# Twelve key-tile steps of row maxima ahead instead of sixteen, in a four-layer graph network on one core

## The reference, cut to what matters

```python
# L2 (adj is 0 or 1 here)
logits = jnp.einsum('bhqd,bhkd->bhqk', q, k) / np.sqrt(DK)
logits = logits + jnp.log(jnp.clip(adj, ADJ_MIN, None))[:, None, :, :]
attn = jax.nn.softmax(logits, axis=-1)
out = jnp.einsum('bhqk,bhkd->bhqd', attn, v)
# L3
logits = jnp.einsum('bhnd,bhmd->bhnm', q, k) / math.sqrt(Hd)
logits = logits + (2.0 * adj - 1.0)
weights = jax.nn.softmax(logits, axis=-1)
weights = weights * (0.25 + 0.75 * adj)
weights = weights / jnp.maximum(weights.sum(axis=-1, keepdims=True), 1e-06)
attended = jnp.einsum('bhnm,bhmd->bhnd', weights, v)
```

## Time and profile before

| | |
|---|---|
| median of 3 runs | 4452.08 us (4448.81 to 4457.96) |
| profiled execution | 4446.08 us, its span 4444.3 us |
| TensorE busy | 4062.8 us, 91% of the span |
| VectorE busy | 3042.6 us, 68% |
| ScalarE, GpSimd busy | 2204.3 us (50%), 1917.8 us (43%) |
| TensorE's granted clock, mean | 0.957 of full speed |

### The profile page before, as it was taken

The page is one execution under the profiler, slowest core; times in us unless marked ns, Lnnn a source line. Parts: engine busy times, 40 slices in busy tenths (PEclk is TensorE's granted clock), DMA queues, the critical chain, the costliest instruction groups (busy, mean ns, idle before and its releaser), DMA issues.

```text
span 4444.3 us, 69344 instructions
## 1 busy us (share of the span) xinstructions
PE 4062.8 (91%) x21040; PEld 2185.1 (49%) x21040; DVE 3042.6 (68%) x5152; ACT 2204.3 (50%) x3894; POOL 1917.8 (43%) x1064
## 2 busy tenths in 40 slices
PE   7998999989999899998999989998999989999898
PEld 6534465344753447543474434744347443574335
DVE  3797746877478764787647876478755787557874
ACT  3365533655336553365534655246543465435663
POOL 1174602746027560265503655036540465404562
PEclk9998999999999999999999999999999999999999
DMA  3201102011020110201112011120111101111010
GB/s 107 77 18 34 51 21 67 18 34 51 25 63 18 34 51 30 60 15 37 48 31 60 16 37 48 34 57 14 39 48 37 53 13 39 50 38 50 11 41 15
DMA packets 106289, 176.57 MB, mean 40 GB/s; under 512 B 27296, under 2 KB 50336, under 8 KB 105888
## 3 DMA queue, kind: packets, MB, share of 16 engines
q1 hardware_dynamic: 105888, 171.69, 13.5%
HBM read 83.12 MB, written 8.39 MB: 21 GB/s over the span
## 4 chain that ended last, share of the span: by engine, by line
PE 58%; issue 15%; POOL 15%; DVE 7%; ACT 3%; SPq 1%; DMA 1%; POOLq 0%; DVEq 0%; ACTq 0%
POOL region_p L1455 11%; PE ps L706 11%; PE ps L565 9%; PE ps L573 9%; PE ps L625 7%; PE ps L675 7%; PE ps L654 7%; PE ps L792 4%; PE ps L614 2%; POOL rstd L1465 1%; SPq L475 1%; DVE region_p L1226 1%; POOL y_t L1516 1%; DVE sums_t L1148 1%; DMA region_k<-region_p 1%
## 5 line engine op out<-in xcount | busy, mean ns | idle before, releaser
L1455 POOL TENSOR_TENSOR region_p<-region_p,mask 128x1024 f32<-128x1024 f32 x608 | 1444.7, 2391 | 427.7 <-ACT region_p L920 426.7
L1196 DVE TENSOR_REDUCE row_max_bf<-ps 128x1 bf16<-128x1024 f32 x768 | 938.9, 1224 | 152.2 <-PE ps L675 133.5
L706 PE MATMUL ps<-region_p,shelf 128*64 128x512 f32 x3584 | 942.8, 597 | 7.8 <-ACT o_raw L943 5.1
L920 ACT ACTIVATE region_p<-ps 128x512 f32<-128x512 f32 x1216 | 660.2, 595 | 407.2 <-PE ps L654 406.3
L654 PE MATMUL ps<-region_q,region_k 97*64 97x512 bf16 x4096 | 685.7, 395 | 2.8
L675 PE MATMUL ps<-region_k,region_q 96*64 96x512 bf16 x3584 | 585.9, 394 | 8.6 <-DVE row_max_bf L1192 8.6
L1182 DVE TENSOR_TENSOR region_p<-ps,mask 128x512 f32<-128x512 f32 x832 | 529.8, 680 | 57.1 <-ACT ps L916 56.6
L1465 POOL TENSOR_TENSOR rstd<-var_eps,minus_half 128x2 f32<-128x2 f32 (+1 forms) x160 | 116.9, 731 | 982.7 <-DVE var_eps L1128 982.7
L916 ACT ACTIVATE ps<-ps 128x512 f32<-128x512 f32 x832 | 446.0, 580 | 178.4 <-PE ps L654 170.2
L654 PEld LDWEIGHTS ps<-region_q,region_k 97*64 97x64 bf16 x4096 | 254.4, 111 | 403.5 <-DVE region_p L1182 129.0
L675 PEld LDWEIGHTS ps<-region_k,region_q 96*64 96x64 bf16 x3584 | 200.4, 112 | 425.9 <-issue 386.8
(11 more groups left out here) (160 smaller groups left out, 5355.5 us busy)
## 6 DMA issues: line engine op xcount, KB each, us to landing
mask<-in_adj SPq DMA_DIRECT2D x64, 512.0 KB, 7.0
mask<-in_adj_t SPq DMA_DIRECT2D x64, 512.0 KB, 3.4
y_t<-o_raw SPq DMA_DIRECT2D x224, 64.0 KB, 2.0
sums_t<-o_raw SPq DMA_DIRECT2D x224, 64.0 KB, 2.0
region_q<-region_p SPq DMA_DIRECT2D x192, 64.0 KB, 2.0
region_k<-region_p SPq DMA_DIRECT2D x192, 64.0 KB, 2.0
region_q<-sums_t SPq DMA_DIRECT2D x192, 64.0 KB, 2.0
region_k<-sums_t SPq DMA_DIRECT2D x192, 64.0 KB, 2.0
```

The costliest lines, as they stand in the source:

```text
L706: last = nc.tensor.matmul(ps[64 * c:64 * c + 64, VALUE_BANK, :], values_and_one, probs[:, t % RING, c * HALF:(c + 1) * HALF], start=(t == ...
L920: nc.scalar.activation(probs[:, t % RING, c * HALF:(c + 1) * HALF], scores_t, ACT.Exp, scale=DK ** -0.5).then_inc(exp_done, 1)
L1196: nc.vector.tensor_reduce(row_max_bf[i][:, t:t + 1], flat[:, (t % 2) * N:(t % 2 + 1) * N], AX.X, ALU.max)\
L1455: nc.gpsimd.tensor_tensor(p, p, mask[:, t, :], ALU.mult).then_inc(masked_pool, 1)
```

## The change: what it does

It sets `AHEAD = 12`. The first part holds 12 lead steps (all of head 0, tiles 0 to 3 of head 1) on three pairs of banks (0 to 5), where a step from step 3 on waits for the step three before it. The remaining 52 steps stand in the main loop 12 steps ahead: at tile t of head h comes step 8h + t + 12. Head 6 therefore has four steps left (head 7's tiles 4 to 7, plain reductions), in its tiles 0 to 3. Rows are transposed at tile 5 (`ROWS_AT`), and SyncE's move of the row stands behind the four moves of `o_raw`. GpSimd masks tiles 0, 2, 4, 5, 7 of heads 0 to 5 instead of 0, 1, 2, 4, 6, and 0, 2, 4, 5 of head 6 instead of 1, 3, 5, 7. The units of the values go to banks 6 and 7 in turn. The scores' ring starts at bank 7, and the first users of banks 4 and 5 wait for all 12 lead steps. Tiles of head 6 masked by VectorE use banks 0 to 3 only from its tile 6 on.

```diff
+AHEAD = 12
+ROWS_AT = 5
-POOL_TILES = {h: (0, 1, 2, 4, 6) for h in range(H - 2)}
-POOL_TILES[H - 2] = (1, 3, 5, 7)
+POOL_TILES = {h: (0, 2, 4, 5, 7) for h in range(H - 2)}
+POOL_TILES[H - 2] = (0, 2, 4, 5)
...
-LEAD_TILES = {h: tuple(range(T)) for h in range(2)}
+LEAD_TILES = {0: tuple(range(T)), 1: tuple(range(AHEAD - T))}
+FIRST_TILES = sum(len(tiles) for tiles in LEAD_TILES.values())
...
-SCORE_BANKS = (4, 5, 7)
+SCORE_BANKS = (7, 4, 5)
...
+def later(h, t):
+
+    at = h * T + t + AHEAD
+    return (at // T, at % T) if at < H * T else None
...
-        late = item[0] == "scores" and item[1] >= H - 2 and item[2] in DVE_TILES[item[1]]
+        late = (item[0] == "scores" and item[1] * T + item[2] >= H * T - AHEAD + 2
+                and item[2] in DVE_TILES[item[1]])
...
+def pair_of(h, t):
+
+    return 2 * ((h * T + t) % 3 if h * T + t < FIRST_TILES else t % 2)
+
+
 def bank_of(name, i):
+
+    if name in ("v2", "v3"):
+        return LIN_BANKS + 2 + i % 2
...
                     for h in range(H):
-                        if h + 2 < H:
-                            max_row(h + 2)
...
+                        if h + 2 < H:
+                            max_row(h + 2)
...
+                    elif BANKS[item] < VALUE_BANK:
+                        pe.wait_ge(max_done, att(b, layer, (0, 0), T, FIRST_TILES))
...
-                    if t == 2 and h < H - 1:
+                    if t == ROWS_AT and h < H - 1:
                         rows_of_maxima(b, layer, h + 1)
-                    if h < H - 2:
-                        scores_for_maximum(b, layer, (0, h + 2), t)
+                    nxt = later(h, t)
+                    if nxt is not None:
+                        scores_for_maximum(b, layer, (0, nxt[0]), nxt[1])
...
+                n = h[1]
+                at = n * T + t
+                if at >= FIRST_TILES:
                     pe.wait_ge(max_done, att(b, layer, h, T, t - 1))
-                n = h[1]
+                elif at >= 3:
+                    pe.wait_ge(max_done, att(b, layer, h, T, t - 2))
+                elif at == 2:
+                    for name in ("q", "k"):
+                        for i in range(2):
+                            wait_emptied(pe, b, name + "23"[layer] + ".1", i)
...
-                for t in range(T):
+                for t in range(AHEAD - T):
                     if t == 2:
                         wait_all_emptied(pe, b, v, 4)
                         rows_of_maxima(b, layer, 0)
```

More of the change, by code:

```diff
@@ L662, in head, with scores_for_maximum @@
                         with_values(b, layer, h - 1, T - LAG + t)
-            def scores_for_maximum(b, layer, h, t, wait=True):
-                if wait:
+            def scores_for_maximum(b, layer, h, t):
+                n = h[1]
+                at = n * T + t
+                if at >= FIRST_TILES:
                     pe.wait_ge(max_done, att(b, layer, h, T, t - 1))
-                n = h[1]
+                elif at >= 3:
[4 more added lines that the diff above has]
+                            wait_emptied(pe, b, name + "23"[layer] + ".1", i)
                 leads = t in LEAD_TILES.get(n, ())
@@ L674, in scores_for_maximum @@
                     for m in range(2):
-                        last = nc.tensor.matmul(ps[64 * m:64 * m + 64, 2 * (t % 2) + c, :],
+                        last = nc.tensor.matmul(ps[64 * m:64 * m + 64, pair_of(n, t) + c, :],
                                                 q_aug[0:AUG - 1, n, t * P + 64 * m:t * P + 64 * m + 64], keys,
@@ L717, in heads @@
                 for t in range(T):
-                    scores_for_maximum(b, layer, FIRST, t, t >= 2)
+                    scores_for_maximum(b, layer, FIRST, t)
                     if t % 2:
@@ L910, in head @@
                         take_sums(b, layer, h - 1)
-                    take_lead(b, layer, h + 2, t)
                     for c in range(2):
@@ L928, in take_lead @@
                     act.wait_ge(diff_done, (b * 2 + layer) * LEADS + leads_before(h, t) + 1)
-                    nc.scalar.activation(lead[:, t % 2, :], ps[:, 2 * (t % 2), :], ACT.Relu).then_inc(lead_ready, 1)
+                    if h * T + t >= 2:
+                        act.wait_ge(max_done, att(b, layer, (0, h), T, t - 1))
+                    nc.scalar.activation(lead[:, t % 2, :], ps[:, pair_of(h, t), :], ACT.Relu).then_inc(lead_ready, 1)
             def take_rows(b, layer, h):
@@ L1173, in head @@
                 for t in range(T):
-                    if h < H - 2:
-                        maximum(b, layer, (0, h + 2), h % 2, t)
+                    nxt = later(h, t)
+                    if nxt is not None:
+                        maximum(b, layer, (0, nxt[0]), nxt[0] % 2, nxt[1])
                     if t in DVE_TILES[h]:
@@ L1191, in maximum @@
                     dve.sem_inc(passed, 1)
-                    nc.vector.tensor_tensor_reduce(lead[:, t % 2, :], lead[:, t % 2, :], ps[:, 2 * (t % 2) + 1, :], 1.0,
+                    nc.vector.tensor_tensor_reduce(lead[:, t % 2, :], lead[:, t % 2, :], ps[:, pair_of(h[1], t) + 1, :], 1.0,
                                                    LOWEST, ALU.add, ALU.max, row_max_bf[i][:, t:t + 1])\
@@ L1195, in maximum @@
                     return
-                nc.vector.tensor_reduce(row_max_bf[i][:, t:t + 1], flat[:, (t % 2) * N:(t % 2 + 1) * N], AX.X, ALU.max)\
+                nc.vector.tensor_reduce(row_max_bf[i][:, t:t + 1], flat[:, pair_of(h[1], t) * HALF:(pair_of(h[1], t) + 2) * HALF], AX.X, ALU.max)\
                   .then_inc(max_done, 1)
```

## The result

The change ran in 4403.02 us (median of 4 runs, 4399.97 to 4407.67), the kernel before in 4451.12 (4 runs). The ratio is 0.9894, with a 95% interval of 0.9882 to 0.9907: 1.1% faster, 48 us, where 12 had been forecast and 4418 was the low end of the range. The profiled execution took 4407.67 us, its span 4405.9; the mean granted clock was 0.970 instead of 0.957. It was the slowest of the four, and the profiled execution of the kernel before, 4446.08 us, was faster than all four of that kernel's runs, so the traces show 38 of the 48 us.

The account below looks back on a forecast made before the run. Limits by regime: bank pairs in the first part, TensorE in heads 1 to 5, VectorE's chain from head 6. Per graph -10.9 + 7.6 + 1.65 = -1.65 us, or -13 in eight: 4440 us against 4452.08, range 4418 to 4470.

Parts of the forecast that it names:

- heads 1 to 5: Main stretch, limited by TensorE: equal counts of work, so no change; a loss of at most 0.9 us per attention.
- The first part and head 0: Start of each attention: four lead steps leave and some lowered clock goes; -5.2 and -5.7 us, -10.9 per graph.
- both bounds: First part, second attention: the gain lies between 4.0 us (four lead steps) and 4.7 (landing of head 0's row).
- A lowered clock in head 6: Head 6: TensorE waits about 1.7 us and the clock falls once per graph, by assumption, costing 1.65 us.
- The clock that comes back with the removed steps: First part and head 0: clock regained with the steps, some 0.6 us in the first attention, 1.7 in the second.
- Head 6 to the end: Four more reductions lengthen VectorE's chain: +3.3 us in the first attention, +4.3 in the second, +7.6 per graph.
- Full clock in head 6: Rival, chance 0.17: no clock is lost in head 6; -26 us over eight graphs, 4426 us.
- Nothing left: Rival, chance 0.24: the clock falls once in each attention, 3.3 us per graph, which takes all the gain; 4452 us.
- slower: Rival, chance 0.21: head 6 leaves TensorE half idle, with a long lowered clock in both attentions; +28 us, 4480.
- head 0's row of maxima: Case within "Nothing left": waiting for this row holds the first scores about 1 us longer in each attention; 4455 us.

Follow-up runs that it names:

- the late quarter: The change with the product of heads 0 to 3 and the last quarter of inverted sums moved behind head 7's mask of tile 2 on VectorE: 4447.94 us.
- the loaded kernel before: The kernel before with nine unread matmuls per attention added in TensorE's waits between head 1's lead steps: 4419.79 us against 4449.45.

## Why the prediction was wrong, point by point

| per graph, us | forecast | measured (the graph of the rows) |
|---|---|---|
| first part, first and second attention | -4.9, -4.3 | -6.5, -4.3 |
| head 0 | -0.3, -1.4 | -0.1, -1.2 |
| heads 1 to 5 | 0, 0 | +0.2, +0.1 |
| head 6 to the end | +3.3, +4.3 | +2.2, +2.9 |
| lowered clock in head 6 | +1.65 | 0 |

Over all eight graphs the rows of the table are on average -5.7 and -4.3, -0.2 and -1.3, +0.1 and +0.1, +2.8 and +3.0, and the lowered clock in head 6 is +0.2, which the +2.8 includes.

*The first part and head 0* came out nearly as their steps said: the first part of the second attention to the tenth and within both bounds, head 0 at 13.7 us where 13.5 was forecast. In the first attention 4.9 was too little. I counted only the lowered stretch behind the transposition as going with the steps; the unit of values at half speed ahead of it, 1.65 us, went too in this graph. In others it stayed: the first part took 15.9 us in most first attentions and 17.5 where the clock was lowered at its start.

*A lowered clock in head 6* is the step that failed: "One per graph is my assumption". In head 6 of this graph TensorE waits 1.72 us once and is busy for 12.38 of 14.10 us, and the clock stays 1.00. So it does in fifteen of the program's sixteen attentions. In the last graph's first attention it fell behind the same wait, 1.81 us there:

```profile
4103.90:4119.70 15.80, 13.99 (x81) 4.97 (x79) 13.65 (x15) 9.20 (x18) 11.54 (x5) 0.89 0.08 18
```

That is 1.7 us more than 14.1, so the price of 1.65 was right and the count was wrong, one in eight graphs. I had likened the wait to those of the lead steps, which are shorter, but there the engine was busy for 4.69 of 6.80 us, and added matmuls cured it. The wait alone does not settle it: with the late quarter the clock fell behind it in six of eight first attentions. What decides there stays open. The Trainium skill ("TensorE: Matmul & The Clock Gate", section "HAM oscillation — how this bites in real kernels") lays the fall of the clock to long waits between bursts of matmuls. The fifteen head 6s agree with it, and it does not explain the lead steps, whose waits were 0.93 us at most.

*The clock that comes back with the removed steps* was sized too low, 0.6 and 1.7 us, 2.3 per graph. The kernel before with added matmuls shows about 3.7 per graph, 11 us more over eight graphs. With the 13 us of the assumed stretch that is most of the 36 us between the forecast and the result.

*Head 6 to the end* was the right mechanism, sized too high: +5.1 instead of +7.6. In the second attention (+2.9 for +4.3) the largest part is the product of heads 0 to 3, which I took over at 2.1 us and which took 1.22, because the new division of head 6's masks lets it start ahead of GpSimd's. I had costed that division at nothing as a mere order. In the first attention +3.0 of the +3.3 is there at head 7's first values, which wait for the copy of o_raw; behind them 0.7 comes back with the clock (0.94 before, 1.00 now). TensorE's four steps are hidden, as I had it.

*The rivals.* Full clock in head 6 was the one that came true in all but one attention, at 0.17, and even its 4426 was too slow by 23. In the graph of the rows head 6 to the end was put 2.5 us too high, and the first attention's first part gained 1.6 us more than forecast. "Nothing left" and "slower" counted a lowered stretch in both attentions of each graph and fell with the assumption; nor did head 0's row of maxima hold the scores.

*Check by another way.* From the loaded kernel before to the change the clock's share is out: 4419.79 to 4403.02, 17 us. The stretches give -4.3 twice in the first part, +0.2 twice in head 0 and +3.0 and +2.9 up to head 7's first values, -2.3 per graph or -18. So by this comparison some 30 of the 48 us are clock and some 17 are steps less head 6. My sum had -0.65 per graph for the clock (-0.6 and -1.7 with the steps, +1.65 in head 6), 5 us in all, and -1.0 for steps less head 6, 8 us.

## What to carry to other kernels

When a stretch runs at a lowered clock, price the clock that its removal gives back in the stages behind it as well as its own. Added matmuls that nobody reads separate the clock from the work in one run; here they gave 30 us without any change to the algorithm. Do not count a lowered stretch for each wait: the same wait in head 6 went with a full clock in fifteen attentions and with a lowered one in the sixteenth. And a lowered clock costs time only where the matmul engine has none to spare: head 0 of the change took 13.7 us at 0.88 and at 1.00. An order of work between two engines that share operands' memory is not free to rearrange: it can halve or double an instruction on a full chain.

## What was not expected of the hardware

Nine idle matmuls per attention made the kernel 0.67% faster.

A product of two operands took 1.22, 2.17 or 2.49 us on VectorE for the same work, by whether and when GpSimd's mask had started ahead of it.

The clock in a stage can differ between versions that do not touch it: with one VectorE instruction moved to head 7 the second attention was as long as in the change, and yet six first attentions began at a clock of 0.90 instead of two, in a first part whose own order had not changed. That kernel was 17 us slower, of which the moved instruction itself explains less than a third. Differences of some 10 us between versions of this kernel are therefore not to be explained by the edited stage alone. Why the stretch fell there was not tried.
